# A three-stage attention and mixture-of-experts kernel: base and expert rows added outside TensorE, weights in pieces, another lead-in

## The chip, the cores and the metric

The kernel runs on one core of a Trainium2 chip. The metric is the time of one execution on the device, in microseconds (us). The core has five engines with an instruction stream each: TensorE (PE; its weight loads are PEld), VectorE (DVE), ScalarE (ACT), GpSimd (POOL) and SyncE (SP), which here only issues DMA transfers. The engines wait for one another by semaphores.

## The reference

```python
def reference(x, Wq, Wk, Wv, Wo, ...):        # x is [32, 256, 128]
    xn = layernorm(x)
    return x + attn(xn) + ffn(xn)

def attn(x):                                   # 32 batch rows, 256 positions, 16 heads of 8
    q, k, v = split_heads(x @ Wq), split_heads(x @ Wk), split_heads(x @ Wv)
    cov = (q - mean(q)) @ (k - mean(k)).T / D
    scores = cov + var(q)[:, None] * var(k)[None, :] / D
    return merge_heads(softmax(scores) @ v) @ Wo

def ffn(x):                                    # here the sequence runs over the 32 batch rows
    x1 = x + causal_attention(layernorm(x)) @ out_proj + b
    hn2 = layernorm(x1)
    gates = top2_of_8(softmax(hn2 @ router.T))
    y = sum over e of (gelu(hn2 @ w1[e]) * gates[e]) @ w2[e]
    return x1 + y
```

## The kernel before, in words

The work has three stages, one after the other, and each engine's instructions are written out in program order by hand.

**Groups** (0 to about 366 us). `run_groups` (L125) runs `group_step(g, r)` for g = -3 to 16 on every engine: the steps -3 to 2 and 11 to 16 are written out, and g = 3 to 10 run in a loop of two turns with four steps each. A group holds 16 positions with their 32 batch rows. In step g an engine does pieces of several groups: causal attention of g, its queries and keys for g+1 and g+2, router, top-2 choice and places of g-1. ScalarE's `hn2T` (L1745) comes once a group. GpSimd scatters the token rows to `token_rows`, ordered by expert (L559, eight indirect DMAs a group), and SyncE stores x1 + x as `out_base`. Between the group pieces stand one-time works: `weight_maximum` on VectorE (L1425), `expert_biases` on TensorE (L1004), `expert_weights` on VectorE (L1445: two passes over 128x2048), clears of block ends and the store of `weight_rows` by SyncE (L1913 and L1953).

**Blocks** (about 392 to 541 us). 40 blocks of 512 rows of one expert each: load by SyncE, two matmul layers on TensorE, store to `expert_out` by GpSimd.

**Steps** (to the end). `step(b, p)` for b = -1 to 32 (`rest_steps` L92, the middle ones in a loop) does 16 heads of attention for batch row b+1, and in between prepares rows b+2 and b+3 and finishes row b-1. step(-1) comes ahead of the blocks. Tables at L43 to L45 say at which head an engine does which extra piece. TensorE is at work on heads all the time: scores from QKT, then probabilities by V. VectorE takes each row's maximum (L1214), ScalarE the exponentials (L1646).

GpSimd's program in a step is, in this order (L634 to L661): `scale_x` (1/std of row b+3, L485), `add_selected` (sum of the two expert rows of b-1, L615), `gather_ready` (L599) and the first `gather` (L610, an indirect DMA from `expert_out` into ysel, called xg in the profile), `features_low` (L519: lower part of the features of b+2, into stack), second gather, `features_squares` (L493: query and key variances of b+3, in four halving sums of `sq`), third gather, `features_high` (L512), fourth gather. What it prepares goes round through other engines: `stack_transposes` on TensorE (L741) transposes `stack`, `project_qk` (L727) multiplies by wqk, `features` on ScalarE (L1613) copies the product to `feat`, and `features_squares` reads that.

`project_out` on TensorE multiplies the merged heads of b-1 by wo and adds two more things in the same PSUM bank, by matmuls with the identity:

```python
for st in range(ST):
    to = misc[0][:, st * P:(st + 1) * P]
    mm(to, oT_all[:, st * P:(st + 1) * P], wo[:], stop=False)
    mm(to, ident[:], base_t[p][:, st], start=False, stop=False)
    ins = mm(to, ident[:], ysel[p][:, 0, st], start=False)
```

`take_output` on ScalarE (L1626) copies the bank to `z_out`, and SyncE stores it. In the order of work around the stages: in group steps 15 and 16 GpSimd prepares rows 0 and 1 (`features_squares(1)` and `features_high(1)` behind the last scatters), step(-1) fills the pipeline of heads, and after the blocks step 0 goes on with it.

## Time and profile before

| | |
|---|---|
| three executions | 1036.33, 1040.39, 1041.9 us; median 1040.39 |
| the profiled execution | 1042.3 us, span 1040.6 us |
| busy | PE 902.4 us (87%), DVE 805.8 (77%), ACT 688.4 (66%), POOL 619.2 (59%) |
| mean granted TensorE clock | 0.934 of full speed |
| DMA | 80.52 MB, mean 77 GB/s |

The span is the stretch of the profile from first to last instruction. Busy counts each engine's own instructions; a wait for a semaphore is idle time. In a row of the time line, the time in square brackets is how long the engine stood idle before the instruction and what released it ("issue": nothing that the profile shows).

### The profile page before, as it was taken

How to read it: one execution, taken by the hardware profiler on the slowest of the kernel's cores; microseconds unless marked ns; L12 is line 12 of the kernel's file. 1: busy time of each engine (PE TensorE's matmuls, PEld its weight loads, DVE VectorE, ACT ScalarE, POOL GpSimd, SP SyncE). 2: the span in 40 equal slices, each digit the busy share in tenths (PEclk: the TensorE clock that was granted, in tenths of full speed). 3: DMA queues.
4: the chain of work that ended last, by engine and by line, in shares of the span. 5: the costliest groups of instructions: out<-in, count | busy, mean ns of one | idle time of the engine just before them, and what ended most of it. 6: DMA issues, size and time to landing. Idle time of an engine off the chain costs nothing.

```text
span 1040.6 us, 34011 instructions
## 1 busy us (share of the span) xinstructions
PE 902.4 (87%) x11962; PEld 564.5 (54%) x11962; DVE 805.8 (77%) x2168; ACT 688.4 (66%) x1395; POOL 619.2 (59%) x886
## 2 busy tenths in 40 slices
PE   3687787888787458999998999999999999999997
PEld 2464554555555325788874555555555555555543
DVE  5878687789888374555566899999999999999880
ACT  3667677778886213443445778778777877787774
POOL 4146475676666662222225777877877777787751
PEclk9678899899999657999997999999999999999998
DMA  6515622122221133777741111111111111111111
GB/s 161 78 32 102 151 67 56 49 68 56 52 64 43 41 112 106 227 224 225 232 139 26 39 44 52 36 49 44 49 39 43 50 37 48 44 49 39 41 47 31
DMA packets 110824, 80.52 MB, mean 77 GB/s; under 512 B 23296, under 2 KB 97920, under 8 KB 110720
## 3 DMA queue, kind: packets, MB, share of 16 engines
q1 hardware_dynamic: 99328, 51.78, 20.3%
q0 software_dynamic: 11392, 27.35, 8.6%
q8 instruction: 66, 1.08, 0.4%
q14 instruction: 38, 0.31, 0.1%
HBM read 44.83 MB, written 33.73 MB: 75 GB/s over the span
## 4 chain that ended last, share of the span: by engine, by line
PE 43%; POOL 19%; issue 14%; DVE 13%; ACT 10%; POOLq 0%; DVEq 0%; DMA 0%; ACTq 0%
PE bank L712 36%; POOL xg L611 4%; POOL stack L523 3%; DVE rowmin L1214 3%; PE bank L751 2%; POOL stack L521 2%; PE bank L1019 2%; POOL rstd L489 2%; POOL sq L501 2%; ACT Vexp L1690 2%; ACT gxb L1718 2%; ACT rows L1733 1%; DVE sprobT L1270 1%; POOL sq L503 1%; POOL token_rows L559 1%
## 5 line engine op out<-in xcount | busy, mean ns | idle before, releaser
L1214 DVE TENSOR_REDUCE rowmin<-bank 128x2 f32<-128x512 f32 x512 | 326.9, 684 | 43.5 <-PE bank L712 43.4
L1646 ACT ACTIVATE prob<-bank 128x512 f32<-128x512 f32 x512 | 290.1, 602 | 81.0 <-PE bank L712 80.6
L712 PE MATMUL bank<-QKT 32*128 32x256 f16 x2048 | 185.0, 277 | 16.1 <-DVE rowmin L1214 12.9
L559 POOL DMA_INDIRECT token_rows<-rows,spots x128 | 127.4, 996 | 40.0 <-issue 31.6
L611 POOL DMA_INDIRECT xg<-expert_out,place x128 | 128.0, 1000 | 33.0 <-POOL spare L607 9.4
L712 PE MATMUL bank<-prob,V 128*25 128x256 f32 x2048 | 137.6, 387 | 0.5 <-ACT prob L1646 0.5
L712 PEld LDWEIGHTS bank<-QKT 32*128 32x128 f16 x2048 | 67.3, 93 | 129.6 <-issue 51.9
L1805 ACT ACTIVATE hmid<-bank,wrow,up_scale 128x512 f32<-128x512 f32 x80 | 58.1, 774 | 88.3 <-PE bank L712 88.3
L631 POOL DMA_DIRECT2D expert_out<-y x40 | 30.2, 755 | 118.7 <-DVE y L1523 111.7
L712 PEld LDWEIGHTS bank<-prob,V 128*25 128x25 f32 x2048 | 50.5, 103 | 52.5 <-issue 27.3
L712 PE MATMUL bank<-wrow,hmid 128*128 128x128 f32 x640 | 78.3, 276 | 0.0
L712 PEld LDWEIGHTS bank<-wrow,hmid 128*128 128x128 f32 x640 | 75.2, 193 | 0.1
L1259 DVE TENSOR_REDUCE smax<-bank 128x16 f32<-128x512 f32 x64 | 43.8, 685 | 30.8 <-PE bank L712 27.5
L712 PE MATMUL bank<-hnT,in_wT 128*128 128x512 f32 x64 | 43.0, 760 | 25.6 <-ACT hnT L1661 22.0
L1513 DVE CAST turned<-bank 128x512 f16<-128x512 f32 x40 | 27.7, 692 | 47.2 <-PE bank L1019 47.2
L712 PE MATMUL bank<-turned,wrow 128*128 128x512 f16 x240 | 60.9, 392 | 3.0 <-DVE turned L1515 3.0
L501 POOL TENSOR_TENSOR sq<-feat 128x512 f32<-128x512 f32 x32 | 33.3, 1041 | 50.4 <-ACT feat L1617 50.4
L712 PE MATMUL bank<-Kexp,gqT 32*32 32x128 f32 x2048 | 40.9, 309 | 15.3 <-issue 15.3
L544 POOL TENSOR_TENSOR rstd<-var,minus_half 128x4 f32<-128x4 f32 x16 | 16.6, 1037 | 60.2 <-DVE minus L1306 60.2
L1270 DVE STREAM_TRANSPOSE sprobT<-prob 128x512 f32<-128x512 f32 x64 | 43.4, 696 | 10.4 <-ACT prob L1697 10.2
L712 PE MATMUL bank<-causal,onesb 128*128 128x512 bf16 x180 | 48.4, 395 | 0.0
L1677 ACT ACTIVATE Kexp<-bank,head_bias,quad_mask 128x512 f32<-128x512 f32 x64 | 44.4, 775 | 5.6 <-PE bank L712 5.6
(227 smaller groups left out, 1918.7 us busy)
## 6 DMA issues: line engine op xcount, KB each, us to landing
xrow<-token_rows SPq DMA_DIRECT2D x40, 258.0 KB, 3.2
wrow<-weight_rows SPq DMA_DIRECT2D x40, 257.0 KB, 3.3
expert_out<-y POOLq DMA_DIRECT2D x40, 256.0 KB, 2.8
token_rows<-xrow SPq DMA_DIRECT2D x16, 258.0 KB
xg<-in_L_attn_x SPq DMA_DIRECT2D x64, 64.0 KB, 2.2
x_in<-in_L_attn_x SPq DMA_DIRECT2D x32, 128.0 KB
out_base<-acc SPq DMA_DIRECT2D x64, 64.0 KB
base_t<-out_base SPq DMA_DIRECT2D x32, 128.0 KB, 2.7
```

The source lines that it names most:

```text
L501: pool.tensor_tensor(sq[:].rearrange(flat), eight, eight, ALU.mult).then_inc(s_pool, 1)
L523: ins = pool.tensor_tensor(slots[p][:, a, :, 2 - a, :], feat[:, a], slots[p][:, a, :, 0, :], ALU.subtract)
L559: pool.indirect_dma_start(token_rows, bass.IndirectOffsetOnAxis(spots[p][:, j:j + 1], 0), rows[p][:, k, t, :].bitcast(U32), None).then_inc ...
L611: pool.indirect_dma_start(ysel[p][:, k, st, :].bitcast(U32), None, expert_out, bass.IndirectOffsetOnAxis(place[p][:, st, k:k + 1], 0)).the ...
L631: pool.dma_start(expert_out[bass.ds(at, BLK), :].rearrange("(s p) e -> p s e", p=P), y_sb[i % YBUFS][:].bitcast(U32)).then_inc(s_yd[i % YB ...
L712: return pe.matmul(o, l, r, start=start, stop=stop, skip_group_check=True)
L1214: dve.tensor_reduce(rowmin[h // 8][:, :, h % TILE_ROWS, h // TILE_ROWS % HALF], row_scores[i % 3][:].rearrange("p (s t) -> p s t", s=ST), ...
L1259: dve.tensor_reduce(smax[:, r, :], ps, AX.X, ALU.max).then_inc(s_dve, 1)
L1270: dve.transpose(sprobT[:, r].rearrange("p h s -> p (h s)"), sprob[:, r].rearrange("p h s -> p (h s)")).then_inc(s_spT[r], 1)
L1646: act.activation(prob[:, h % 8].rearrange("p t s -> p (t s)"), col_scores[h % 2][:], ACT.Exp, scale=exp_register).then_inc(s_exp, 1)
L1677: ins = act.activation(Kexp[:, :, j, :], head_bank[:].rearrange("p (n t) -> p n t", n=GPOS), ACT.Identity, bias=head_bias[:, j:j + 1], sca ...
L1805: act.activation(hmid[i % 2][c][:], up_bank[c][:], ACT.Gelu, bias=w[:, c:c + 1], scale=up_scale[:, 0:1]).then_inc(s_mid, 1)
```

## The change

1. **Steps.** TensorE's four matmuls with the identity are gone from `project_out`, and its waits for the base and the expert rows with them. GpSimd gets `add_base`: the base is added to the first expert row, after `features_squares` and ahead of the third gather; `add_selected` adds the second row in the next step as before. `take_output` moves from ScalarE to VectorE, at head 14, and adds the sum to the projection there. `gather_ready` waits for the output of two rows back instead of its projection, SyncE's base load for `add_selected`.
2. **Groups.** VectorE, ScalarE, GpSimd and SyncE have all group steps written out (`every_group`); TensorE keeps its loop. `weight_maximum` goes from step 0 to -1, `expert_biases` ahead of `causal_pv(0)`; `expert_weights` is done for one expert in each of steps 2 to 9, the clears of ends one a step in 2 to 9, and `weight_rows` is stored in eight transfers in steps 4 to 11. In steps -2 and -1 TensorE gets matmuls whose results nobody reads (`first_warm`, `keep_warm`).
3. **Seams.** Row 1 is prepared earlier: `scale_x(1)` in step 14, `normalise_x(1)`, its transposes, `project_qk(1)`, `features(1)` within step 15, GpSimd's squares, high and low parts of row 1 ahead of `scatter(15, 0)`. `half_out(0, 0, 0)` and the transposes that it needs come later, in step 16. Behind the last block TensorE does four matmuls that nobody reads. Step 0 on GpSimd does `features_low` directly behind `features_high` and issues only its two first gathers; step 1 begins with `add_base(0)` and the two others.

```diff
-DVE_AT = dict(half1=1, out=5, half0=10, statistics=0, shift1=12, shift0=3)
+DVE_AT = dict(half1=1, out=5, half0=10, statistics=0, shift1=12, shift0=3, output=14)
...
+def every_group(step):
+
+    for g in range(-3, GROUPS + 1):
+        step(g, g % 4)
...
-                if isinstance(g, int) and g == GROUPS - 1:
                     scale_x(1)
                 if ahead:
                     scales(g + 3)
                 if tail:
                     add_x(g, r)
+                    if isinstance(g, int) and g == GROUPS - 1:
+                        features_squares(1)
+                        features_high(1)
+                        features_low(1)
                     scatter(g, p, 0)
...
-                    pool.wait_ge(s_pr_ps, n - 1)
+                    pool.wait_ge(s_z, n - 1)
...
+            def add_base(n, p):
+                pool.wait_ge(s_based[p], n * 8 + (16 - 8 * p))
+                pool.wait_ge(s_sel[p], n * 32 + (32 - 32 * p))
+                pool.tensor_tensor(ysel[p][:, 0], ysel[p][:, 0], base_t[p][:], ALU.add).then_inc(s_pool, 1)
+                pool.wait_ge(s_pool, own.next())
...
                 if norm:
                     scale_x(b + 3)
-                if prev:
+                if second:
+                    add_base(b - 1, 1 - p)
+                    gather(1 - p, 1, 0)
+                    gather(1 - p, 1, 1)
+                if prev and not second:
                     add_selected(b - 1, 1 - p)
-                if cur and not first:
+                if cur and not early:
                     gather_ready(b, p)
                     gather(p, 0, 0)
-                if prep and not first:
+                if prep and not early and not second:
                     features_low(p)
-                if cur and not first:
+                if cur and not early:
                     gather(p, 0, 1)
+                if second:
+                    add_selected(b - 1, 1 - p)
                 if norm:
                     features_squares(b + 3)
-                if first:
+                if cur and not early:
+                    add_base(b, p)
+                    gather(p, 1, 0)
+                if norm:
+                    features_high(1 - p)
+                if early:
+                    features_low(1 - p)
+                if cur and early:
                     gather_ready(b, p)
                     gather(p, 0, 0)
                     gather(p, 0, 1)
-                if cur:
-                    gather(p, 1, 0)
-                if norm:
-                    features_high(1 - p)
-                if cur:
+                if cur and not early:
                     gather(p, 1, 1)
...
-            run_groups(pool, group_step)
-            features_squares(1)
-            features_high(1)
+            every_group(group_step)
             step(-1, 1)
-            features_low(0)
...
-                pe.wait_ge(s_ysum, b + 1)
-                pe.wait_ge(s_based[p], b * 8 + (16 - 8 * p))
                 for st in range(ST):
                     to = misc[0][:, st * P:(st + 1) * P]
-                    mm(to, oT_all[:, st * P:(st + 1) * P], wo[:], stop=False)
-                    mm(to, ident[:], base_t[p][:, st], start=False, stop=False)
-                    ins = mm(to, ident[:], ysel[p][:, 0, st], start=False)
+                    ins = mm(to, oT_all[:, st * P:(st + 1) * P], wo[:])
                 ins.then_inc(s_pr_ps, 1)
...
+                    keep_warm(g, 5)
+                if isinstance(g, int) and g == GROUPS:
+                    pe.wait_ge(s_feat, 2)
+                    stack_transposes(0, 0, 0)
                 if late:
                     router_logits(g - 1)
+                if isinstance(g, int) and g == 0:
+                    expert_biases()
...
-                    if isinstance(g, int) and g == 0:
-                        expert_biases()
                     keep_warm(g, 4)
                 if isinstance(g, int) and g == GROUPS - 2:
                     xn_transposes(0, 0)
                 if isinstance(g, int) and g == GROUPS - 1:
-                    stack_transposes(0, 0, 0)
+                    xn_transposes(1, 1)
+                if isinstance(g, int) and g == -2:
+                    first_warm(14)
+                if isinstance(g, int) and g == -1:
+                    keep_warm(g, 8)
...
+                if isinstance(g, int) and g == GROUPS - 1:
+                    project_qk(1, 1)
...
-                if isinstance(g, int) and g == GROUPS - 1:
-                    xn_transposes(1, 1)
...
+            def first_warm(times):
+
+                pe.wait_ge(s_ident, 2)
+                pe.wait_ge(s_zeroed, 1)
+                for i in range(times):
+                    mm(seq_bank[0][:], identh[:], stack[0][:].rearrange("p a s h k -> p (a s h k)")[:, 0:512])
...
                 expert_down(BLOCKS - 1)
+                for i in range(4):
+                    mm(row_scores[2][:], onesb[:], causal[:].rearrange("k h t -> k (h t)"))
...
+            def take_output(b, p):
+                dve.wait_ge(s_pr_ps, b + 1)
+                dve.wait_ge(s_ysum, b + 1)
+                if positive(b * 8 - 8 * p):
+                    dve.wait_ge(s_out[p], b * 8 - 8 * p)
+                dve.tensor_tensor(z_out[p][:], misc[0][:, 0:NS].rearrange("p (s e) -> p s e", s=ST), ysel[p][:, 0],
+                                  ALU.add).then_inc(s_z, 1)
...
-                if isinstance(g, int) and g == GROUPS:
-                    half_out(0, 0, 0)
...
+                    weight_maximum()
                 if tail:
                     score_maxima(g, 3)
                     if isinstance(g, int) and g == 0:
-                        weight_maximum()
...
                     block_numbers()
+                    half_out(0, 0, 0)
...
+                if isinstance(g, int) and g == 1:
+                    expert_scales()
+                if isinstance(g, int) and 2 <= g < 2 + NE:
+                    expert_weights(g - 2)
...
+            def expert_weights(e):
+                dve.tensor_scalar(wts[:, e, 0:FF], w1_sb[:, e], w1_scale[:, 0:1], None, ALU.mult).then_inc(s_dve, 1)
+                dve.wait_ge(s_dve, own.next())
+                dve.scalar_tensor_tensor(out=wts[:, e, FF:2 * FF], in0=w1_sb[:, e], scalar=w1_scale[:, 0:1],
+                                         in1=wts[:, e, 0:FF], op0=ALU.mult, op1=ALU.subtract).then_inc(s_setup, 1)
...
-            def take_output(b, p):
-                act.wait_ge(s_pr_ps, b + 1)
-                if positive(b * 8 - 8 * p):
-                    act.wait_ge(s_out[p], b * 8 - 8 * p)
-                act.copy(z_out[p][:].rearrange("p s e -> p (s e)"), misc[0][:, 0:NS]).then_inc(s_z, 1)
...
-                if isinstance(g, int) and g == GROUPS:
-                    features(1)
+                if isinstance(g, int) and g == GROUPS - 1:
+                    normalise_x(1, 1)
...
-                    sp.wait_ge(s_pr_ps, b - 1)
+                    sp.wait_ge(s_ysum, b - 1)
...
-                if isinstance(g, int) and g == 2:
-                    clear_ends()
-                    sp.wait_ge(s_setup, 3)
-                    sp.wait_ge(s_dma_w2, 16 * FC)
-                    sp.dma_start(weight_rows.rearrange("(e p) c -> p e c", p=P), wts[:].bitcast(U32)).then_inc(s_wput, 16)
+                if isinstance(g, int) and 2 <= g < 2 + NE:
+                    clear(NE * CAP + (g - 2) * BLK)
+                if isinstance(g, int) and 4 <= g < 4 + NE:
+                    put_weights(g - 4)
...
+            def put_weights(e):
+                sp.wait_ge(s_setup, 2 + e + 1)
+                sp.wait_ge(s_dma_w2, 16 * FC)
+                sp.dma_start(weight_rows[e * P:(e + 1) * P, :], wts[:, e].bitcast(U32)).then_inc(s_wput, 16)
```

GpSimd in a loop step, from the squares to the last gather of the step (xg is ysel; s_sel counts gathers that have landed, s_based base loads). Before:

```order
L501 TENSOR_TENSOR sq<-feat 128x512 [waits s_half_ps1]
L503 TENSOR_TENSOR sq<-sq 128x64x4 [waits s_pool]
L506 TENSOR_TENSOR sq<-sq 128x64x2 [waits s_pool]
L509 TENSOR_TENSOR sq<-sq 128x64 [waits s_pool]
L611 DMA xg<-expert_out,place 128x128 [waits s_pool]
L513 TENSOR_SCALAR feat<-sq,var_scale 128x64
L516 CAST stack<-feat 128x64x9 [waits s_pool]
L611 DMA xg<-expert_out,place 128x128 [waits s_pool]
```

And with the change:

```order
L507 TENSOR_TENSOR sq<-feat 128x512 [waits s_half_ps1]
L509 TENSOR_TENSOR sq<-sq 128x64x4 [waits s_pool]
L512 TENSOR_TENSOR sq<-sq 128x64x2 [waits s_pool]
L515 TENSOR_TENSOR sq<-sq 128x64 [waits s_pool]
L625 ISA [waits s_pool]
L626 REGISTER_ALU [waits s_based1]
L627 TENSOR_TENSOR xg<-xg,base_t 128x256 [waits s_sel1]
L620 DMA xg<-expert_out,place 128x128 [waits s_pool]
L519 TENSOR_SCALAR feat<-sq,var_scale 128x64
L522 CAST stack<-feat 128x64x9 [waits s_pool]
L620 DMA xg<-expert_out,place 128x128 [waits s_pool]
```

One addition on 128x256 has come in between the squares and the third gather, with two waits of its own, and the gather waits for it.

GpSimd from the scatters of group 15 to the first rows of step(-1), before:

```order
L559 DMA token_rows<-rows,spots 73728x129 x3
L574 ISA
L559 DMA token_rows<-rows,spots 73728x129 x4
L501 TENSOR_TENSOR sq<-feat 128x512 [waits s_feat]
L503 TENSOR_TENSOR sq<-sq 128x64x4 [waits s_pool]
L506 TENSOR_TENSOR sq<-sq 128x64x2 [waits s_pool]
L509 TENSOR_TENSOR sq<-sq 128x64 [waits s_pool]
L513 TENSOR_SCALAR feat<-sq,var_scale 128x64 [waits s_pool]
L516 CAST stack<-feat 128x64x9 [waits s_pool]
L637 ISA [waits s_pool]
L489 TENSOR_TENSOR rstd<-var_x,minus_half 128x2 [waits s_xn,s_var]
L491 TENSOR_TENSOR centre<-minus_mean,rstd 128x2 [waits s_pool]
```

And with the change:

```order
L507 TENSOR_TENSOR sq<-feat 128x512 [waits s_feat]
L509 TENSOR_TENSOR sq<-sq 128x64x4 [waits s_pool]
L512 TENSOR_TENSOR sq<-sq 128x64x2 [waits s_pool]
L515 TENSOR_TENSOR sq<-sq 128x64 [waits s_pool]
L519 TENSOR_SCALAR feat<-sq,var_scale 128x64 [waits s_pool]
L522 CAST stack<-feat 128x64x9 [waits s_pool]
L527 COPY stack<-stack 128x32x9 [waits s_pool]
L527 COPY stack<-stack 128x32x9
L529 TENSOR_TENSOR stack<-feat,stack 128x32x9 x2
...
L565 DMA token_rows<-rows,spots 73728x129 [waits s_pool]
L565 DMA token_rows<-rows,spots 73728x129 x3
...
L565 DMA token_rows<-rows,spots 73728x129 x4
L652 ISA
L495 TENSOR_TENSOR rstd<-var_x,minus_half 128x2 [waits s_xn,s_var]
```

The squares, high and low parts of row 1 stand ahead of the scatters, and scale_x(2) (L495) follows the last scatter directly.

TensorE's output projection in a late step, up to the transposes of a shift, before:

```order
L712 MATMUL bank<-wo,oT_all 128x128 [waits s_ysum,s_based0,s_oa,s_half0]
L712 MATMUL bank<-base_t,ident 128x128
L712 MATMUL bank<-xg,ident 128x128
L712 MATMUL bank<-wo,oT_all 128x128
L712 MATMUL bank<-base_t,ident 128x128
L712 MATMUL bank<-xg,ident 128x128
L834 MATMUL bank<-identh,shift 16x128 [waits s_shift1,s_sht0]
```

And with the change:

```order
L734 MATMUL bank<-wo,oT_all 128x128 [waits s_oa,s_half0]
L734 MATMUL bank<-wo,oT_all 128x128
L852 MATMUL bank<-identh,shift 16x128 [waits s_shift1,s_feat]
```

Four matmuls have gone, and with them the waits for s_ysum and s_based.

## Rows read from the trace of the kernel before

**Rows 1.** Stretches: span, busy us (records) per engine, clock, DMA share, GB/s.
```profile
392.50:541.00 148.50, 145.48 (x1040) 115.72 (x1040) 82.30 (x119) 59.42 (x81) 30.82 (x43) 0.96 0.64 195
541.00:586.00 45.00, 38.90 (x397) 19.86 (x396) 33.95 (x76) 28.83 (x61) 26.14 (x41) 0.81 0.14 39
586.00:1000.00 414.00, 402.65 (x4811) 222.04 (x4807) 378.74 (x815) 322.37 (x708) 322.67 (x489) 1.00 0.17 44
```

**Rows 2.** Time line of one step: start, us, engine, line, operation, [idle <- releaser].
```profile
801.68 1.04 POOL L501 TENSOR_TENSOR sq<-feat 128x512 f32<-128x512 f32 x1 [1.23 <-ACT feat L1617]
...
802.80 0.72 POOL L503 TENSOR_TENSOR sq<-sq 128x256 f32<-128x256 f32 x1
...
803.59 0.39 PE L712 MATMUL bank<-base_t,ident 128*128 128x128 f32 x2
803.61 0.40 POOL L506 TENSOR_TENSOR sq<-sq 128x128 f32<-128x128 f32 x1
803.81 0.39 PE L712 MATMUL bank<-xg,ident 128*128 128x128 f32 x2
...
810.04 0.72 POOL L617 TENSOR_TENSOR xg<-xg 128x256 f32<-128x256 f32 x1 [0.64 <-DMA xg<-expert_out,place]
...
813.10 1.41 POOL L523 TENSOR_TENSOR stack<-feat,stack 128x288 f16<-128x288 f32 x2
...
814.57 0.45 PEld L751 LDWEIGHTS bank<-identh,stack 128*128 128x128 f16 x8 [0.42 <-POOL stack L523]
...
816.15 0.59 ACT L1617 COPY feat<-bank 128x512 f32<-128x512 f32 x1 [0.71 <-PE bank L712]
...
816.89 1.04 POOL L501 TENSOR_TENSOR sq<-feat 128x512 f32<-128x512 f32 x1 [1.23 <-ACT feat L1617]
```

**Rows 3.** Waits of 620 to 1000: us in total, times, longest.
```profile
POOL sq L501 <- ACT feat L1617: 30.7, 25, 1.2
```

**Rows 4.** VectorE's L1237 in 620 to 1000: duration ns min/median/max, starts, form.
```profile
L1237 DVE TENSOR_TENSOR o_nat<-bank,rsum x25: 423/425/426, 630.6 to 994.0; 128x256 f32<-128x256 f32 x25
```

**Rows 5.** Time line of the group stage: VectorE, TensorE and ScalarE's hn2T.
```profile
33.61 2.27 DVE L1429 TENSOR_REDUCE w_max<-w_sb 128x1 f32<-128x2048 f32 x1
...
50.38 4.61 PE L712 MATMUL bank<-ln2b,w_sb 128*128 128x1 f32 x32
...
60.03 0.77 ACT L1745 ACTIVATE hn2T<-bank,ln2b,ln2w_top 128x512 f32<-128x512 f32 x1
...
71.86 2.35 DVE L1454 SCALAR_TENSOR_TENSOR wts<-w_sb,w_scale,wts 128x2048 f16<-128x2048 f32 x1
...
79.35 2.07 PE L712 MATMUL bank<-hnT,in_wT 128*128 128x512 f32 x2 [4.53 <-ACT hnT L1661]
...
114.71 1.95 PE L712 MATMUL bank<-Kexp,gqT 32*32 32x128 f32 x70 [4.14 <-issue]
...
242.56 0.77 ACT L1745 ACTIVATE hn2T<-bank,ln2b,ln2w_top 128x512 f32<-128x512 f32 x1
...
260.38 0.77 ACT L1745 ACTIVATE hn2T<-bank,ln2b,ln2w_top 128x512 f32<-128x512 f32 x1
...
359.21 0.76 ACT L1745 ACTIVATE hn2T<-bank,ln2b,ln2w_top 128x512 f32<-128x512 f32 x1
```

**Rows 6.** Time line of TensorE ahead of the blocks.
```profile
383.06 0.69 PE L724 MATMUL bank<-ident,xn 128*128 128x128 f32 x2 [4.09 <-ACT shiftT L1653]
```

**Rows 7.** Clock: two stretches of 6 us, and TensorE in them.
```profile
228.00:234.00 6.00, 4.42 (x155) 3.49 (x156) 3.97 (x16) 2.88 (x8) 4.03 (x6) 1.00 0.36 86
565.00:571.00 6.00, 2.31 (x25) 1.29 (x22) 2.88 (x5) 3.58 (x9) 4.88 (x10) 0.78 0.26 67
...
230.74 1.74 PE L712 MATMUL bank<-Kexp,gqT 32*32 32x128 f32 x96 [1.46 <-issue]
...
570.56 1.01 PE L751 MATMUL bank<-identh,stack 128*128 128x128 f16 x8 [2.48 <-POOL stack L523]
571.36 2.02 PE L712 MATMUL bank<-wqk,xnT 128*128 128x256 f32 x4
```

43 lines of the change are left out of this document (20 added, 23 removed).

## The prediction

> **What bounds the kernel now.** I read the stretches first, then the time line and the chain of one steady step, the wait totals, and last the stalls of the groups and of the seams. The stretches give stages with different limits: the blocks (TensorE busy 145.5 of 148.5 us) and the steps [rows 1], and the groups before them. From 586 to 1000 us TensorE is busy 402.7 of 414.0 us and VectorE 378.7, GpSimd only 322.7, so by shares TensorE looks like the bound of the steps and GpSimd like an engine with a fifth of its time free. The time line of one step says otherwise. GpSimd's squares start at 801.68 and again at 816.89 [rows 2]; over many steps the period is 15.13 us. Between them lies a closed loop: squares, a gather, high parts, a gather, scale_x, add_selected, a gather, low parts (L523, over at 814.51), then TensorE's stack transposes at 814.57, which had waited 0.42 us for just that L523, then the wqk matmuls, ScalarE's copy to feat at 816.15, and squares again, which waited 1.23 us for that copy. All but about 2.4 us of the loop is GpSimd's program in its own order. Each of 25 steps shows the same wait of 1.2 us before the squares [rows 3], and that is GpSimd's idle time: it cannot be filled, since it is the way round through the other two engines. Before add_selected stand another 0.64 us, for a gather [rows 2]. So two limits lie close together: the GpSimd loop at 15.13, and TensorE, which has 0.4 us of slack a step.
>
> **The steps.** The change adds add_base to GpSimd in each step, between squares and the next gather, inside that loop. The trace has the same operation on the same shape: add_selected (L617), 0.72 us [rows 2]. It also waits for its own completion before the gather is issued; dependent operations of the squares start 0.81 us apart for 0.72 of work (802.80 to 803.61) [rows 2], so 0.08 more. That gives 0.80 us a step. The base load and the two gathers that it waits for have been issued before squares begin, so I cost that wait at nothing; if the gather is late it costs up to the 0.64 us that add_selected waits for its own. TensorE loses four of the six matmuls of project_out: they start 0.22 us apart (803.59, 803.81) [rows 2], so 0.89 us a step. VectorE gets the output addition, 128x256 from PSUM, for which normalise_out's row has 0.424 us [rows 4]; ScalarE loses its copy, which nothing waited for. gather_ready now waits for the output of two steps back, long over: nothing. The second half of the question is whether the loop feels TensorE's relief. It does not: the transposes start when L523 ends, and TensorE merely arrives there earlier and waits about 1.7 us in place of 0.42, as VectorE would let it: its share [rows 1] is 13.8 us a step, 14.3 with the addition. From both sides: below, if TensorE were the limit, the step would shrink by 0.5 to 0.7; above, the whole 0.80 plus a late gather, 1.44. I take 0.80, because the same wait stands in every step. The loop runs for the 27 steps that still make low parts behind the base addition, 27 x 0.80 = **+21.6 us**. The last steps have no features; there TensorE's own chain counts and the projection is shorter: two steps by 0.9 and the last, at the lower clock, by 1.2: **-3.0 us** (-2.0 to -3.5).
>
> The Trainium skill, "GPSIMD Engine Reference", section 4.1, speaks against this part: it puts a two-input elementwise addition on VectorE and calls GpSimd about 2x slower. Here the two rows have 0.72 [rows 2] against 0.42 us [rows 4], 1.7x. By the page's factor, as an estimate from it, the addition would be 0.85 us and the steps would lose 3 us more than I say.
>
> **The groups.** ScalarE's hn2T starts at 60.03 for group 0 and 359.21 for group 15; two undisturbed neighbours are 17.82 apart (242.56, 260.38) [rows 5], and others that nothing disturbs run up to 18.5; I take 18.2. Fifteen of them are 273 us against 299.2 spent, so 26 us are disturbances, and a few more lie ahead of group 0. By what the change does to each: (a) weight_maximum, 4.5 us on VectorE at 33.61 in the midst of group 0, moves to an idle place a group earlier, and expert_biases, 4.61 us on TensorE at 50.38 [rows 5], moves ahead of causal_pv, with matmuls that fill TensorE in the first groups and may hold its clock: -8.0 (-4 to -10). (b) expert_weights in one piece holds VectorE for 2.35 us in its second half alone, at 71.86, and TensorE then waited 4.53 at 79.35 [rows 5]; an eighth of both is under 0.5 us: -5.2, and the eight pieces give back 1.6 (0 to 3.5). (c) Eight clears and the whole weight store go out together in group 2; behind them TensorE waited 4.14 us for instructions at 114.71 [rows 5]; in eight small transfers over eight groups: -7.2 for groups 2 and 3 (-3 to -8). (d) Four engines lose the loop and its return at about 177 us, TensorE keeps its own: -3.7 for the return in the middle (0 to -5), an estimate from what is left of the 26 us when the others are taken off. Sum **-22.5 us**, range -10 to -28. Each of these stalls is met on TensorE or ScalarE, which carry the group; where one goes, the next limit is the undisturbed 18.2.
>
> **The seams.** After the last group GpSimd scatters, then does squares and high parts of batch row 1, and only then scale_x(2), for which TensorE's transposes waited 4.09 us at 383.06 [rows 6]. The features now stand ahead of the last scatters, 4.4 us earlier work on an engine that is ahead of its work there, at the price that the scatters may start 0.7 late: **-3.6 us** (-2 to -6). Behind the blocks, TensorE's clock is at the lower level for the first heads (0.81 in the mean over 541 to 586 [rows 1]). Four added matmuls cover the short wait for the last y, and features_low comes earlier in step 0: **-2.4 us** (0 to -3.7).
>
> **Sum.** +21.6 - 3.0 - 22.5 - 3.6 - 2.4 = -9.9 us. The profiled execution took 1042.3 us (span 1040.6), 1.9 over the median of the three, so 1032.4 by its own time and 1030.5 by the median. I say **1032 us**. A measurement can tell about 0.5% here, 5.2 us.
>
> **Rivals.** *The clock falls in the steps, and the kernel is slower.* TensorE now stands still for about 1.7 us before each stack transposes. In the trace the granted clock is 1.00 (2.4 GHz) over the 6 us around a single stall of 1.46 us at 230.74, and 0.78 over the 6 us that end with a stall of 2.48 us at 570.56 [rows 7]. At the lower level (1.2 GHz) the transposes and wqk then took 2.8 us, from 570.56 to 573.38 [rows 7], instead of 1.6 [rows 2], and both are in the loop, so a fall may cost up to 1.2 us a step. It outweighs the sum from 8 falls on: in a third of the steps, +11, 1043; in nearly all, +24 to +32, 1056 to 1064. For it: the stall is longer than any that the clock is seen to survive. Against: it is one stall, with TensorE busy around it. *TensorE and VectorE are the bound after all.* Then steps go down to 14.5 us, 27 x -0.6 = -16 instead of +21.6: 994. Only the shares speak for it; the wait before squares in every step speaks against. *The group stage gives half.* The stalls for instructions come from elsewhere than the stores and the loop, TensorE's return still holds up everyone, and the pieces cost more than they save: -11 instead of -22.5: 1043. *The addition waits.* add_base finds its gather late and everything in the loop slides by 1.2 to 1.4 us: 27 x 0.5 = +13, 1045. That the change does not do what it says I leave out, since the order of instructions shows each part.
>
> **Chances.** The forecast 0.40 (of this 0.33 faster by over 0.5%, 0.07 within); clock in part or nearly all of the steps 0.30 (0.02 / 0.13 / 0.15); half the group gain 0.14 (0.02 / 0.07 / 0.05); addition late 0.08 (0 / 0.04 / 0.04); TensorE the bound 0.08 (all faster). Together faster 0.45, same 0.31, slower 0.24. The range from 1014 (group gain and seams at their best, loop 0.6) to 1055 (the clock falls in two of three steps) leaves out the TensorE case and the worst of the clock's, about 0.17.
>
> **What would show it.** Right: squares 15.9 us apart, add_base 0.72 us directly behind them, TensorE idle 1.5 to 1.9 us for GpSimd's L529 at the stack transposes, VectorE idle more than before, the granted clock at full speed; hn2T of group 15 near 337; the blocks starting near 366. Wrong: squares 15.1 apart or less (the loop had slack), or 17 with a granted clock below 1.00 between 600 and 1000; hn2T of group 15 later than 348, with a stall for instructions on TensorE in the middle groups; a wait on a gather before add_base.

## The result: slower, where faster was forecast

The changed kernel took 1068.65 us (median of four, 1056.15 to 1069.76) against 1038.36 for the kernel before (four, 1036.01 to 1041.9). The ratio is 1.0261, with a 95% interval from 1.0177 to 1.0346: slower by 2.6%, clear of the 0.5% that can be told. The forecast was 1032, with 1014 to 1055 as its range and 0.24 for slower. The profiled execution took 1069.43 us, its span is 1067.8. Three executions of the experiments ran in a slower state and count in the medians below but not in the ratios: 1924.95 us with three matmuls in the stall, 1510.03 us with the sum moved, and 1091.18 us of the slowest kernel.

The profile after has these shares and slices on its page (the slices are tenths of 40 equal parts of the span):

```profile
PE 904.9 (85%) x11728; PEld 541.9 (51%) x11745; DVE 830.9 (78%) x2214; ACT 685.5 (64%) x1363; POOL 640.5 (60%) x918
...
PEclk9899988989997589999999988988989988989987
```

TensorE is busy as long as before (902.4 us), though about 30 steps have lost four matmuls each. The row PEclk gives a reason: in the steps it was 9 nearly throughout before, and now 8 stands among the nines. At a lower clock the same matmuls are busy longer. The stretches say it in numbers (columns as in [rows 1]):

```profile
392.50:541.00 148.50, 146.60 (x1164) 113.65 (x1163) 93.11 (x151) 68.33 (x105) 37.16 (x54) 1.00 0.62 191
541.00:586.00 45.00, 36.25 (x435) 18.98 (x432) 36.49 (x78) 29.84 (x66) 34.86 (x52) 1.00 0.18 47
586.00:1000.00 414.00, 375.48 (x4096) 188.72 (x4092) 354.86 (x758) 288.51 (x608) 305.67 (x461) 0.91 0.15 40
```

Over the steps the granted clock is 0.91 of full speed against 1.00 [rows 1]. GpSimd's squares, one a step, show how the steps went (time line of GpSimd, squares alone):

```profile
567.31 1.04 POOL L507 TENSOR_TENSOR sq<-feat 128x512 f32<-128x512 f32 x1 [1.23 <-ACT feat L1669]
...
634.54 1.04 POOL L507 TENSOR_TENSOR sq<-feat 128x512 f32<-128x512 f32 x1 [2.27 <-ACT feat L1669]
...
651.46 1.04 POOL L507 TENSOR_TENSOR sq<-feat 128x512 f32<-128x512 f32 x1 [2.14 <-ACT feat L1669]
...
738.83 1.04 POOL L507 TENSOR_TENSOR sq<-feat 128x512 f32<-128x512 f32 x1 [3.79 <-ACT feat L1669]
...
754.87 1.04 POOL L507 TENSOR_TENSOR sq<-feat 128x512 f32<-128x512 f32 x1 [1.23 <-ACT feat L1669]
...
770.91 1.04 POOL L507 TENSOR_TENSOR sq<-feat 128x512 f32<-128x512 f32 x1 [1.22 <-ACT feat L1669]
...
1009.66 1.04 POOL L507 TENSOR_TENSOR sq<-feat 128x512 f32<-128x512 f32 x1 [2.07 <-ACT feat L1669]
```

Before, the squares were 15.1 us apart and always waited 1.23 us for feat [rows 2, 3]. Now there are three kinds of step: 16.04 us with the old wait of 1.2 us (754.87 to 770.91), about 17 with a wait of 2.2 us (634.54 to 651.46), and two of 18.7 with 3.8 us (one at 738.83). From 567.31, the third squares behind the blocks, to the last at 1009.66, 26 periods take 442.35 us, 17.01 each, against 394.06 or 15.16 in the kernel before. That is where the time went:

| from, to | before | after | difference |
|---|---|---|---|
| start to hn2T of group 15 | 359.21 | 343.28 | -15.9 |
| from there to the first block | 33.29 | 32.40 | -0.9 |
| first block to squares(5), the third behind the blocks | 197.27 | 191.63 | -5.6 |
| 26 steps | 394.06 | 442.35 | +48.3 |
| from there to the end of the span | 56.77 | 58.14 | +1.4 |
| sum | 1040.6 | 1067.8 | +27.2 |

The time line of one of the longer steps, with the stretches of 2 us around it (clock in the column behind POOL), shows what lengthens it:

```profile
784.66 0.62 PE L773 MATMUL bank<-identh,stack 128*128 128x128 f16 x8 [1.58 <-POOL stack L529]
...
785.12 1.90 PE L734 MATMUL bank<-wqk,xnT 128*128 128x256 f32 x4
```
```profile
782.00:784.00 2.00, 1.07 (x12) 0.49 (x11) 2.00 (x4) 2.00 (x5) 1.99 (x5) 1.00 0.35 69
784.00:786.00 2.00, 1.34 (x11) 1.17 (x12) 0.83 (x2) 0.08 (x1) 1.60 (x2) 0.81 0.33 100
786.00:788.00 2.00, 2.00 (x15) 0.80 (x17) 0.49 (x2) 0.95 (x2) 0.20 (x1) 0.50 0.13 33
```

and TensorE in a step of the shorter kind, with GpSimd ahead of it:

```profile
757.27 0.31 POOL L515 TENSOR_TENSOR sq<-sq 128x64 f32<-128x64 f32 x1
...
757.83 0.74 POOL L627 TENSOR_TENSOR xg<-xg,base_t 128x256 f32<-128x256 f32 x1 [0.25 <-POOL sq L515]
...
758.84 0.98 POOL L620 DMA_INDIRECT xg<-expert_out,place  x1 [0.27 <-POOL xg L627]
...
767.14 1.40 POOL L529 TENSOR_TENSOR stack<-feat,stack 128x288 f16<-128x288 f32 x2
...
768.68 0.61 PE L773 MATMUL bank<-identh,stack 128*128 128x128 f16 x8 [1.65 <-POOL stack L529]
...
769.12 1.08 PE L734 MATMUL bank<-wqk,xnT 128*128 128x256 f32 x4
```

In both, TensorE stands about 1.6 us for GpSimd's L529 ahead of the stack transposes, as against 0.42 [rows 2]. In the short step the wqk matmuls take 1.08 us. In the long one the clock falls right behind the stall, to 0.50 over 786 to 788, and the same four matmuls take 1.90. Feat, for which GpSimd's squares wait, comes that much later, and the loop is 1 us longer.

That is only half of the falls. A fall behind such a stall, and in the step after it one without:

```profile
614.15 0.69 PE L773 MATMUL bank<-identh,stack 128*128 128x128 f16 x8 [1.44 <-POOL stack L529]
...
627.80 0.27 PE L852 MATMUL bank<-identh,shift 128*16 128x128 f16 x2 [0.56 <-DVE shift L1263]
...
632.30 0.62 PE L773 MATMUL bank<-identh,stack 128*128 128x128 f16 x8
```
```profile
626.00:628.00 2.00, 1.23 (x12) 0.65 (x10) 1.93 (x5) 1.91 (x4) 1.18 (x4) 1.00 0.03 8
628.00:630.00 2.00, 2.00 (x22) 0.66 (x20) 1.97 (x5) 0.88 (x3) 1.99 (x4) 0.56 0.12 18
```

Between 600 and 1000 us the granted clock fell to 0.50 nineteen times, for 3.5 to 7.5 us each. Ten falls began right behind the stall ahead of the stack transposes. The nine others came 13 to 14 us after one of these, where TensorE had stood only 0.5 to 0.7 us for a shift of VectorE (627.80); TensorE's work then ran slowly until the transposes were due, and at 632.30 it had no stall left. And the length of the stall alone does not decide: the clock fell behind 1.44 us at 614.15 and stayed up behind 1.65 us at 768.68, 1.55 at 752.54, 1.62 at 956.59 and 1.72 at 990.46.

The wait totals (us in total, times, longest) of 620 to 1000:

```profile
POOL sq L507 <- ACT feat L1669: 47.6, 22, 3.8
...
PE bank L773 <- POOL stack L529: 21.2, 13, 1.8
...
PEld bank L773 <- POOL stack L529: 18.9, 10, 1.9
...
POOL xg L627 <- POOL sq L515: 5.6, 22, 0.3
```

Squares wait 47.6 us in 22 waits, before 30.7 in 25 [rows 3]. TensorE's matmuls wait 21.2 us for L529, 13 times, 1.6 us each, where it was 0.42 us before [rows 2]; the PEld row has the weight loads of ten of the same stalls, and is not added. `add_base` (L627) waits for the squares alone in these steps, so the rival in which the addition finds its gather late did not come. Outside them it waited 1.7 to 2.8 us for a gather or the base load, once at 544.81 and three times from 1025.99 on; whether that cost anything is not shown.

### The profile page after: what moved, and what is told of

Same layout as the page of the kernel before. It is cut to its first block, busy times and chain, and to the rows that moved or that the text cites. A ratio compares the mean times of both kernels' runs of the same rounds, so it can differ in the third digit from the quotient of the medians.

```text
span 1067.8 us, 33399 instructions
## 1 busy us (share of the span) xinstructions
PE 904.9 (85%) x11728; PEld 541.9 (51%) x11745; DVE 830.9 (78%) x2214; ACT 685.5 (64%) x1363; POOL 640.5 (60%) x918
## 4 chain that ended last, share of the span: by engine, by line
PE 37%; POOL 23%; issue 15%; DVE 13%; ACT 10%; DMA 1%; SPq 1%; POOLq 1%; DVEq 0%; ACTq 0%
PE bank L734 32%; POOL xg L620 4%; DVE rowmin L1253 3%; POOL stack L529 3%; ACT Vexp L1736 2%; POOL sq L507 2%; PE bank L773 2%; PE bank L1056 2%; POOL stack L527 2%; POOL sq L509 2%; POOL stack L522 2%; ACT gxb L1764 1%; POOL token_rows L565 1%; POOL xg L627 1%; POOL rstd L495 1%
## 5 line engine op out<-in xcount | busy, mean ns | idle before, releaser
L1692 ACT ACTIVATE prob<-bank 128x512 f32<-128x512 f32 x512 | 286.9, 599 | 94.5 <-PE bank L734 93.5
L734 PE MATMUL bank<-QKT 32*128 32x256 f16 x2048 | 196.4, 287 | 23.5 <-DVE rowmin L1253 17.4
L734 PE MATMUL bank<-prob,V 128*25 128x256 f32 x2048 | 150.3, 415 | 0.0
L734 PEld LDWEIGHTS bank<-prob,V 128*25 128x25 f32 x2048 | 53.3, 109 | 60.2 <-issue 39.5
L773 PE MATMUL bank<-identh,stack 128*128 128x128 f16 x512 | 42.0, 228 | 31.5 <-POOL stack L529 31.5
L1244 DVE COPY QKT<-bank 128x1024 f16<-128x1024 f16 x64 | 43.7, 683 | 27.1 <-PE bank L773 23.4
L1669 ACT COPY feat<-bank 128x512 f32<-128x512 f32 x32 | 18.8, 586 | 62.5 <-PE bank L734 62.5
L734 PE MATMUL bank<-hnT,in_wT 128*128 128x512 f32 x64 | 37.0, 661 | 20.4 <-ACT hnT L1707 15.4
L773 PEld LDWEIGHTS bank<-identh,stack 128*128 128x128 f16 x512 | 30.4, 101 | 46.8 <-issue 24.3
```

Source lines behind the costliest of these rows:

```text
L734: return pe.matmul(o, l, r, start=start, stop=stop, skip_group_check=True)
L773: ins = pe.transpose(m[:, a, g, st], stack[p][:, a, st, h:h + TILE_ROWS, :].rearrange("p h k -> p (h k)"), identh[:])
L1244: dve.tensor_copy(QKT[p][:, :, HALF * k:HALF * (k + 1), :], misc[0][:].bitcast(F16).rearrange("p (a g s) -> p a g s", a=2, g=HALF)).then_i ...
L1692: act.activation(prob[:, h % 8].rearrange("p t s -> p (t s)"), col_scores[h % 2][:], ACT.Exp, scale=exp_register).then_inc(s_exp, 1)
```

## The experiments

All changes are against the kernel after the change unless another is named. Theory A was: a step is as long as GpSimd's loop, and the fallen clock comes on top, caused by TensorE's stall. Theory B: the added work on VectorE and GpSimd takes the time itself, and the clock only follows. Each group of four ran with the kernel before on the same chip, which took 1034.25, 1034.87 and 1035.58 us there.

**Matmuls in the stall.** In `step` of TensorE, ahead of `stack_transposes(b + 2, p, 0)`; six of them, and in a second kernel three:

```diff
+                        if prev:
+                            for i in range(6):
+                                mm(misc[0][:], onesb[:], causal[:].rearrange("k h t -> k (h t)"))
                         stack_transposes(b + 2, p, 0)
```

> The kernel after the change, with six 128x512 matmuls of constants put on TensorE in each step ahead of the stack transposes that wait for GpSimd's low parts; their results are overwritten. About 0.2 us each at full clock, so 1.3 us of the 1.6 us stall is filled with work and the chain through GpSimd is untouched. Theory A (a step is 15.93 us by GpSimd's loop, and about 1.1 us more because the clock falls in the stall): the granted clock stays at full speed from 600 to 1000 us, squares come 15.9 to 16.0 us apart instead of 17.0, and the time falls by 26 x 1.1 = 28 us, to about 1040. Theory B (the extra microsecond is the new work on VectorE and GpSimd, and the clock only follows): the period stays at 17 or grows, 1067 or more.

> The same with three matmuls, 0.65 us. Theory A: the stall that is left is about 1.0 us, shorter than those through which the clock stayed up in the kernel before, so nearly as good as six, 1040 to 1048. If the clock asks for more than that, a mixture of steps of 16 and 17 us, about 1055. Theory B: 1067.

With six 1045.5 us (1.0114 of before, 1.0069 to 1.0159), with three 1045.62 (1.0085, 1.0045 to 1.0125). Nothing was taken away, work was added, and the median fell by 23 us. (The ratios differ by less, 1.5 to 1.8%: on this chip the kernel before was 4 us faster too, and one of the four executions of the changed kernel took only 1056.15 us; its mean clock was 0.928, that of the others 0.911 to 0.917.) The stretch 600 to 940 us of the kernel with six and with three, and two squares of the former:

```profile
600.00:940.00 340.00, 327.64 (x3694) 162.37 (x3691) 299.74 (x658) 245.20 (x530) 265.88 (x403) 1.00 0.16 42
```
```profile
600.00:940.00 340.00, 313.22 (x3606) 156.24 (x3604) 298.74 (x654) 244.29 (x527) 266.79 (x402) 1.00 0.16 43
```
```profile
710.08 1.04 POOL L507 TENSOR_TENSOR sq<-feat 128x512 f32<-128x512 f32 x1 [1.23 <-ACT feat L1672]
...
726.12 1.04 POOL L507 TENSOR_TENSOR sq<-feat 128x512 f32<-128x512 f32 x1 [1.15 <-ACT feat L1672]
```

The clock is 1.00 in both; the squares are 16.08 us apart with six (26 periods) and 16.06 with three. Against 17.01 this is 24 us in 26 steps, as much as the medians differ. Theory A holds, B falls. The falls of the clock without a long stall before them are gone too, so they hung on the others; how, no run shows. With three matmuls a stall of up to 0.9 us was left. They do as well as six: how much of the stall has to be filled I did not look for further.

**Projection as before.** `project_out`, `take_output` and their waits as in the kernel before, no `add_base`; groups, pieces, lead-in and warm matmuls as changed:

```diff
                 if cur and not early:
-                    add_base(b, p)
                     gather(p, 1, 0)
...
-                    ins = mm(to, oT_all[:, st * P:(st + 1) * P], wo[:])
+                    mm(to, oT_all[:, st * P:(st + 1) * P], wo[:], stop=False)
+                    mm(to, ident[:], base_t[p][:, st], start=False, stop=False)
+                    ins = mm(to, ident[:], ysel[p][:, 0, st], start=False)
```

> The kernel after the change, but base and expert rows go back to TensorE's projection and the copy back to ScalarE, as before; groups, weights in pieces, lead-in and the warm matmuls stay as changed. Theory A: steps of 15.13 us as before at full clock, and what groups and seams brought remains: squares(3) came 22.1 us earlier in the changed kernel, so about 1040 - 22 = 1018 us. If groups and seams brought that only in one execution or cost later, nearer to 1035.

1017.27 us, ratio 0.9814 (0.9771 to 0.9857), squares 15.13 us apart. So the other two parts of the change gain 1.9% by the ratio, 17 us by the medians, and by the ratios (0.9814 and 1.0261) the new output path costs 4.5%, 46 us.

**The loop alone.** The same kernel with `add_base` kept on GpSimd as well, so that the base is added twice to the output:

> The kernel with groups and seams as changed and TensorE's projection as before, to which GpSimd's add_base is given as well, so that the base is added twice. GpSimd's loop is as long as in the changed kernel, TensorE keeps its four matmuls. Theory A: period 15.93 to 16.05 by the loop. TensorE's stall is then 0.9 us shorter than in the changed kernel, about as with three or four filling matmuls, so the clock stays up: 1017 + 27 x 0.9 = 1041. This prices the loop alone. Theory B (what costs is the relief of TensorE or VectorE's new work): period near 15.1, 1018. If a stall of about 1.2 us already lets the clock fall, 17.0 and 1066.

1047.73 us (1.0132, 1.0067 to 1.0197), squares 16.11 us apart, clock 1.00 from 600 to 940. This is the price of add_base in the loop with nothing else: 0.98 us a step against 15.13. It also bears on the clock: with the four matmuls kept, TensorE waits at most 0.4 us for L529 between 620 and 940 us, and the clock stays up. Without add_base it stays up even when they are gone, as the kernel with the base on VectorE shows below. It is the two together, the longer loop and the cheaper projection, that make the stall. By the traces, the cheaper projection made the step longer, 17.01 us against 16.11; the intervals of the two ratios (1.0261 and 1.0132) touch, and `take_output` is on ScalarE here, which is not taken apart.

**TensorE's groups written out.** `run_groups(pe, group_step)` becomes `every_group(group_step)`:

> The kernel after the change, with TensorE's group steps written out too. In the changed kernel TensorE stood 1.96, 3.44 and 1.90 us for instructions at 132.73, 169.71 and 214.13, and the groups around those are 4 to 5.5 us longer. If these stalls belong to the loop (its return at 169.71, its code for the others), they go, hn2T of group 15 comes 10 to 14 us earlier than 343.3, and the time falls by the same, to about 1055. If they belong to the stretch of code fetched and not to the loop, the stalls stay or move, and the time stays at 1065 to 1069.

1056.07 us (1.0212, 1.0152 to 1.0271). The median is 12 us below that of the changed kernel, but the intervals of the ratios overlap, so the traces have to say it: hn2T of group 15 came at 335.90, 7.4 us earlier, and the steps took 16.69 us in place of 17.01, since fewer of them met the low clock in that execution. In the changed kernel three stalls of TensorE had no cause that the profile shows, and the group around the first ran at a lower clock (the group from 190.04 on is one without such a stall):

```profile
132.73 0.40 PE L734 MATMUL bank<-causal,seq_eye 32*128 32x512 bf16 x4 [1.96 <-issue]
...
169.71 1.12 PE L734 MATMUL bank<-hnT,in_wT 128*128 128x512 f32 x2 [3.44 <-issue]
...
214.13 0.40 PE L734 MATMUL bank<-causal,seq_eye 32*128 32x512 bf16 x4 [1.90 <-issue]
```
```profile
126.42:148.37 21.95, 17.14 (x329) 11.95 (x329) 15.99 (x65) 15.24 (x31) 12.16 (x14) 0.84 0.30 74
190.04:207.87 17.83, 14.82 (x329) 9.94 (x329) 16.75 (x67) 15.16 (x31) 12.46 (x15) 1.00 0.38 91
```

Written out, the stall at 169.71 is gone, and its group takes 17.7 us in place of 23.5. The other two long groups stay, 21.9 and 21.5 us: stalls of 1.4 and 1.7 us stand at 134.21 and 138.49, and of 1.4 and 1.3 at 228.21 and 232.34. So only the one in the middle belonged to the loop, and hn2T gained 7.4 us where 10 to 14 had been expected; what the others come from stays open.

**The sum of the expert rows in the wait for feat.** `add_selected` goes from ahead of the first gather to directly ahead of the squares:

```diff
-                if prev and not second:
-                    add_selected(b - 1, 1 - p)
                 if cur and not early:
                     gather_ready(b, p)
...
-                if second:
+                if prev:
                     add_selected(b - 1, 1 - p)
                 if norm:
                     features_squares(b + 3)
```

> The kernel after the change, with add_selected moved from ahead of the first gather to directly ahead of the squares, into the 1.2 us in which GpSimd waits for feat. Its own gather has then long landed, so 0.64 us of wait and 0.72 us of work leave the loop: 15.95 - 1.4 = 14.5 us, no longer above what VectorE (14.3) and TensorE (14.2) need, so the stall before the transposes and with it the clock's fall go too. Theory A: squares 14.5 to 14.8 us apart, 1067 - 26 x 2.4 = about 1005. Theory B (the bound is the work of the added operations on VectorE or the order of heads): no better than 1055.

1013.27 us (0.9794, 0.9747 to 0.9841), clock 1.00, squares 15.02 us apart: by one move 55 us below the changed kernel's median, 4.7% by the ratios. The step did not come down to 14.5 to 14.8. The time lines of GpSimd and TensorE in this kernel show what still bounds it:

```profile
694.70 1.03 POOL L620 DMA_INDIRECT xg<-expert_out,place  x1 [0.49 <-POOL spare L616]
...
698.04 0.62 PE L771 MATMUL bank<-identh,stack 128*128 128x128 f16 x8 [0.53 <-POOL stack L529]
...
700.36 1.04 POOL L507 TENSOR_TENSOR sq<-feat 128x512 f32<-128x512 f32 x1 [0.47 <-ACT feat L1667]
```

TensorE still waits for L529 and the squares still wait for feat, so it is GpSimd's loop as before. The move took 1.03 us out of it and not 1.4: from the start of scale_x's last operation (L497) to the start of the next gather it is 0.86 us here and 1.89 in the changed kernel. The gather that `add_selected` had waited for cost 0.55 us there and not 0.64, and the wait ahead of the next gather has grown from 0.28 to 0.49.

**The same move in the kernel before.**

> The kernel before the change, with that same move of add_selected and nothing else. Theory A: the loop falls from 15.13 to about 13.8 and TensorE with its 14.7 us of work becomes the bound: 14.8 us a step, 27 x 0.3 = 8 us less, 1026 to 1030 beside 1035 for the kernel before. If TensorE were the bound before already, no change. If moving the sum later delays the projection, which waits for it, slower.

1055.13 us, ratio 1.0204 (1.0165 to 1.0243): slower by 20 us, where I had expected a gain of 8. The clock is 1.00, squares are 15.79 us apart and wait 2.2 us for feat; TensorE did not wait for GpSimd. Time line of one step of this kernel:

```profile
704.78 1.04 POOL L611 DMA_INDIRECT xg<-expert_out,place  x1 [0.50 <-POOL spare L607]
...
705.36 0.65 DVE L1222 TENSOR_SCALAR shift<-rowmin 128x16 f16<-128x16 f32 x1
...
705.84 0.88 POOL L521 COPY stack<-stack 128x288 f16<-128x288 f16 x2
...
706.04 0.71 DVE L1224 SCALAR_TENSOR_TENSOR shift<-rowmin,shift 128x16 f16<-128x16 f32 x1
...
706.69 1.41 POOL L523 TENSOR_TENSOR stack<-feat,stack 128x288 f16<-128x288 f32 x2
...
706.89 0.27 PE L834 MATMUL bank<-identh,shift 128*16 128x128 f16 x2 [0.83 <-DVE shift L1224]
```

L1222 and L1224 are two operations on 16 elements in each partition. They took 0.65 and 0.71 us here, while GpSimd was issuing a gather and copying; by groups of lines (busy us, mean ns) over 620 to 940, first before, then with the move:

```profile
L1224 DVE SCALAR_TENSOR_TENSOR shift<-rowmin,shift 128x16 f16<-128x16 f32 x43 | 18.9, 439 | 1.5
...
L1222 DVE TENSOR_SCALAR shift<-rowmin 128x16 f16<-128x16 f32 x43 | 7.6, 176 | 1.5
```
```profile
L1224 DVE SCALAR_TENSOR_TENSOR shift<-rowmin,shift 128x16 f16<-128x16 f32 x40 | 28.0, 700 | 1.4
...
L1222 DVE TENSOR_SCALAR shift<-rowmin 128x16 f16<-128x16 f32 x40 | 15.9, 397 | 1.4
```

Their means went from 176 and 439 ns to 397 and 700. With two of each a step, that is 2 x (0.221 + 0.261) = 0.96 us, and TensorE waits for their result (0.83 us at 706.89). The wait totals of 620 to 1000 have this wait 24 times, and for the kernel before they have none on a shift:

```profile
PE bank L834 <- DVE shift L1224: 19.6, 24, 1.1
```

TensorE is busy 318.7 of 340 us from 600 to 940, 14.8 us a step, as in the kernel before (332.0 of 340). These 14.8, the 0.8 of waiting for shifts and the 0.2 for row minima make the 15.8 measured. The Trainium skill, "SBUF — State Buffer", section "SBUF: two separate sides", has VectorE and GpSimd share a pair of ports to SBUF as an exclusive lock, for whole instructions, which certain VectorE operations need (those with two inputs from SBUF among them, against a GpSimd operation that reads SBUF). The rows agree as far as they go: L1222 took 0.17 us in the kernel before and 0.65 at 705.36, and L1224 0.71 at 706.04, until GpSimd's copy beside it was over. That the move changed the meeting of the two is shown; that nothing else did it is not.

**Projection as before, TensorE written out, with the move and without.**

> Groups and seams as changed, projection and output as before the change, TensorE's groups written out, add_selected moved into the wait for feat. Sum of the parts: 1017 (projection as before) - 8 to -12 (TensorE's loop) - 8 (move) = about 1000.

> Groups and seams as changed, projection and output as before the change, TensorE's groups written out, add_selected where it was. The difference to the slow kernel of 1079 us is the place of add_selected alone. If that place caused the collisions in the steps, squares are 15.1 us apart at full clock and the time is 1017 - 7 = about 1009. If the unrolling changes the phase of the steps by itself, 1030 or more.

With the move 1079.42 us (1.0388, 1.0309 to 1.0468), the slowest of all, where about 1000 had been expected; in its profiled execution, 12 us above the median with 1091.18, the steps took 18.2 us at a clock of 0.87 over 600 to 940. VectorE's two small operations for the shift took 657 and 713 ns in the mean there, and TensorE waited for them 27.4 us in 21 times (longest 1.5), with the falls of the clock behind these waits. Without it 1013.56 (0.9769, 0.9722 to 0.9815), 15.1 us a step for all but one, and the two operations took 189 and 426 ns. The place of one 0.72-us operation decides over 6%, in opposite directions for the two ways to make the output.

**The base on VectorE.** `add_base` gone from GpSimd, a second addition in `take_output`, which now waits for the base load; SyncE's next base load waits for the output:

```diff
                 dve.tensor_tensor(z_out[p][:], misc[0][:, 0:NS].rearrange("p (s e) -> p s e", s=ST), ysel[p][:, 0],
-                                  ALU.add).then_inc(s_z, 1)
+                                  ALU.add).then_inc(s_dve, 1)
+                dve.wait_ge(s_dve, own.next())
+                dve.tensor_tensor(z_out[p][:], z_out[p][:], base_t[p][:], ALU.add).then_inc(s_z, 1)
```

> The kernel after the change, but the base is added on VectorE, right after the output addition (a second 128x256 addition), and add_base is gone from GpSimd. Theory A: the loop through GpSimd is as long as before the change, 15.13 us, and TensorE's stall before the transposes about 0.9 us, so the clock stays up: 1067 - 26 x 1.9 = 1018. VectorE needs 14.3 + 0.5 = 14.8 us, just under the loop. Theory C (VectorE is the next bound as soon as it has this): 15.3 or more, 1025. If the addition waits out GpSimd's own work, 1 us more on VectorE, 15.8 and 1035.

1017.39 us (0.9799, 0.9750 to 0.9848), squares 15.16 us apart, clock 1.00 from 600 to 940: the loop's old length and nothing on top. The stall of 0.9 us that I had expected is not there; TensorE waits for L529 only 3 times from 620 to 940, at most 0.2 us.

**Without the four matmuls behind the blocks**, on the kernel with the projection as before:

> The kernel with groups and seams as changed and projection and output as before (1017 us), without the four matmuls behind the last block that nobody reads. If they keep the clock up through the wait for the last y, as the prediction said, the clock falls behind the blocks as in the kernel before and squares(3) come 2 to 3 us later after the first block: 1020. If the clock would stay up anyway, no change, 1017.

1020.33 us (0.9822, 0.9765 to 0.9880), an interval that holds the 0.9814 of the kernel with them. In the profiled executions squares(3) came 161.9 us behind the first block, with the matmuls 160.8. TensorE stood 0.79 us for the last y, and with them it did not. But the clock fell soon behind the blocks either way, from 533 to 540 us with them and from 531.5 to 542.5 without. If they gain anything, it is about 1 us; this stays unclear.

**The best of these.** The sum in the wait for feat and TensorE's groups written out:

> The kernel after the change, with add_selected moved into the wait for feat and TensorE's group steps written out. Both were measured alone: the move gave 1008 to 1014 us with squares 15.01 us apart, the unrolling brought hn2T of group 15 forward by 7.4 us. If the two are independent: 1000 to 1006. If the unrolled TensorE comes to the steps in another phase against GpSimd, so that the clock falls or both small shift operations of VectorE meet GpSimd's work, as in the kernel with projection as before, unrolled and moved sum (steps of 16.4 to 20): 1040 or more.

1004.7 us, ratio 0.9703 (0.9661 to 0.9745), 3% below the kernel before and more than 5% below the changed one, with squares 15.03 us apart and a clock of 1.00 from 600 to 940. The new output path, which cost 46 us where it was put, is in it.

## Why the prediction was wrong

**The loop: right.** That GpSimd's loop bounds the step although TensorE is busy 97% of it, that TensorE's relief gains nothing, that TensorE then waits 1.6 us at the stack transposes (1.7 forecast): all as said. The term was 0.80 us and is 0.90 to 0.98. What was missing stands in the rows of the step: 1.26 us from the end of L515 (757.58) to the next gather (758.84), where 0.27 us had been the wait before. Of the difference of 0.99 the wait of 0.25 ahead of the addition was not in my sum (I had one handshake, there are two), and 0.09 comes back because the next sum waits less for its gather (0.55 against 0.64). So +25 us for 27 steps instead of +21.6. One sentence on the loop was wrong: that GpSimd's wait of 1.2 us for feat cannot be filled. The moved sum fills most of it, and the wait falls to 0.47 us.

**The clock: this is the step that failed.** The sum has no term for the clock; it took the granted clock as 1.00 in all steps, and over 586 to 1000 us it was 0.91. The forecast took this case as the likeliest (0.40) and gave 0.30 to the rival, half of that to its slow end, which came: it had priced a fall in nearly all steps at 1056 to 1064 us and up to 1.2 us a step. The runs show 0.93 us a step (17.01 against 16.08 with the stall filled), 24 us. The evidence that I weighed was right and spoke for the rival: the stall of 1.6 us is longer than the longest through which the clock was seen to stay up, 1.46 us [rows 7]. "It is one stall, with TensorE busy around it" was no evidence, since the 1.46 us were one stall too. The rival itself was simpler than the trace: it knew one fall a step, behind the stall, and the trace has falls behind it and others a step later, with stalls of 1.44 us that went with a fall and of 1.72 that did not. Where a forecast hangs on a step beyond anything observed, the likelier side is the one beyond.

**The groups: right in kind, too large.** -15.9 us at hn2T of group 15 instead of -22.5, and within the range given. The periods without a disturbance are 17.5 to 18.7 us as forecast, and the two long ones of weights and stores have gone. But three new ones of 22 to 23.5 us stand where TensorE stalls for nothing that the profile shows. The term "(d)", the loop's return, was taken as a gain of 3.7 and gained nothing, because TensorE kept its loop: its stall of 3.44 us at 169.71 went only when the loop did. The long groups around the other two stayed even then.

**The seams: half right.** Ahead of the blocks -0.9 us instead of -3.6. scale_x(2) comes 12.1 us after the last scatter places are known (`spots`) instead of 15.2, near the 3.7 forecast, though the scatters start 1.5 us later behind `spots` than before and not 0.7. But the places now come 8.6 us behind hn2T instead of 6.5. VectorE's and GpSimd's time lines of the changed kernel show it:

```profile
345.84 1.28 POOL L574 TENSOR_TENSOR acc<-x,xg 128x512 f32<-128x512 f32 x1
...
345.95 2.22 DVE L1366 TENSOR_TENSOR ldiff<-top 128x32 f32<-128x32 f32 x1
...
347.06 1.05 POOL L507 TENSOR_TENSOR sq<-feat 128x512 f32<-128x512 f32 x1
```

L1366 works on 32 elements a partition and took 0.19 us before; here it took 2.22, from just behind the start of GpSimd's addition on x until the squares behind it were over as well (348.1). I had costed the features put ahead of the scatters by GpSimd's time alone, and not by what they do to VectorE beside them. Behind the blocks -5.6 us up to squares(5) instead of -2.4, and of this the four matmuls explain at most about 1 us; the rest I did not take apart. The last part of the kernel gained nothing (+1.4 instead of -3.0).

**The sum in one line:** groups -15.9, seams -6.5, loop +24, clock +24, end +1.4 make +27. Of the forecast's error of 37 us the clock is 24. The other 13 are groups 6.6, end 4.4 and loop 2.5, less 0.5 for the seams: without the clock's fall the kernel takes 1045 us, no clear gain either, as the two kernels with the filled stall show.

## What to carry to other kernels

A closed loop through several engines bounds a kernel even when the engine that does most of it has a fifth of its time free: look for the wait that returns with the same length in every period, and put new work of that engine into that wait (the sum moved there brought 4.7%), and then look at what the work now runs beside: in the kernel before the same move cost 2%. Taking work off TensorE where it is not the bound turns busy time into a stall, and the stall can cost the clock: ask for the longest single stall that results, not only for the sum of the work. Where the loop has to be longer, matmuls that nobody reads, put into the stall, bought the clock back here.

## What the runs showed of the hardware

- Between 600 and 1000 us the granted clock fell to 1.2 GHz behind ten of fourteen single stalls of 1.44 to 1.77 us; four of 1.55 to 1.72 us kept it. Nine more falls came 13 to 14 us later, behind waits of 0.5 to 0.7 us. It stayed up throughout 600 to 940 us when three 128x512 matmuls stood in the stall.
- VectorE's operations on 16 or 32 elements a partition took 0.17 to 0.19 us at best and 0.65 to 0.73, once 2.22 us, beside GpSimd's work. For such an operation on which TensorE waits, what GpSimd does at that moment cost more than the operation itself.
- Two kernels whose GpSimd program differs in the place of one addition of 0.72 us ran 15.1 and 18.2 us a step in their profiled executions, 1013.56 and 1079.42 us by the medians. What is gained in one engine's loop can be lost by where its work then falls beside the others.
